# GLA joined to the attention and feed-forward block: one memory map, no barrier, its first steps beside the last feed-forward supertiles

## What is computed

```python
x = x + ln(attention(ln(x), qkv_w, qkv_b, out_w, out_b))
x = x + ln(ffn(ln(x), ternary(W1), b1, ternary(W2), b2))
x = x + ln(gla(ln(x), Wq, Wk, Wv, Wo, Wg, Wog, Wd, bd, norm_w))
x = x + ln(experts(ln(x), gate_W, W1, b1, W2, b2, Ws1, bs1, Ws2, bs2))

# inside gla: 16 heads of 64, sequences of 1024 tokens
log_decay = -softplus(x @ Wd.T + bd)
k_gated   = (x @ Wk.T) * sigmoid(x @ Wg.T)
s_t = exp(g_t) * s_{t-1} + k_t^T v_t ;  o_t = q_t s_t
out = rmsnorm(o) * norm_w * sigmoid(x @ Wog.T)  @ Wo.T
```

## Time and profile before

| | |
|---|---|
| median of 3 runs | 2134.86 us (2133.71 to 2137.86) |
| the profiled execution | 2135.97 us |
| its span in the trace | 2133.8 us |
| mean granted PE clock | 0.966 |
| PE / PEld busy | 94% / 66% |
| DVE / ACT / POOL busy | 71% / 60% / 28% |
| DMA | 176.5 MB, 83 GB/s on average |

### The profile page before, as it was taken

How to read it: one execution, slowest core, us unless ns; L and a number is a source line. 1 busy time by engine, 2 the same in 40 slices (tenths; PEclk the granted TensorE clock), 3 DMA queues, 4 the chain that set the end, 5 groups by cost and what they waited for, 6 DMA issues and landing times. The chain is left out here.

```text
span 2133.8 us, 42103 instructions
## 1 busy us (share of the span) xinstructions
PE 1996.7 (94%) x16914; PEld 1412.3 (66%) x16914; DVE 1519.0 (71%) x2461; ACT 1289.1 (60%) x2555; POOL 597.0 (28%) x481
## 2 busy tenths in 40 slices
PE   7999999999999997983899999999999999589997
PEld 6643333333333346972788888888888888478996
DVE  7889999999999966974465655555565554467774
ACT  3258888888888865763454545454545454255664
POOL 1200000000000024541333343434343433124454
PEclk9889999999999999995999999999999999879999
DMA  6732232232232222205212131212221212132221
GB/s 227 247 54 64 65 71 69 59 77 70 52 84 71 68 69 70 70 31 152 90 62 85 59 99 62 88 61 80 62 80 62 80 62 70 43 107 97 112 110 70
DMA packets 99410, 176.53 MB, mean 83 GB/s; under 512 B 24120, under 2 KB 61776, under 8 KB 94096
## 3 DMA queue, kind: packets, MB, share of 16 engines
q1 hardware_dynamic: 99216, 173.84, 26.8%
HBM read 134.35 MB, written 38.67 MB: 81 GB/s over the span
## 5 line engine op out<-in xcount | busy, mean ns | idle before, releaser
L731 DVE TENSOR_REDUCE att_sb_mx<-att_ps_psM 128x1 f32<-128x1024 f32 x512 | 624.1, 1221 | 27.6 <-PE att_ps_psM L944 24.9
L1149 ACT ACTIVATE att_sb_pt<-att_ps_psSO 128x512 f32<-128x512 f32 x1024 | 557.1, 597 | 94.5 <-PE att_ps_psSO L962 39.6
L944 PE MATMUL att_ps_psM<-stack_sb_k,stack_sb_q 48*128 48x512 f32 x1024 | 382.4, 455 | 4.9 <-DVE att_sb_mx L731 3.3
L962 PE MATMUL att_ps_psSO<-stack_sb_q,stack_sb_k 50*128 50x512 f32 x1024 | 373.5, 444 | 0.0
L974 PE MATMUL att_ps_psSO<-att_sb_pt,stack_sb_v 128*32 128x256 f32 x4096 | 326.4, 391 | 8.6 <-ACT att_sb_osb L1142 8.6
L962 PEld LDWEIGHTS att_ps_psSO<-stack_sb_q,stack_sb_k 50*128 50x128 f32 x1024 | 153.1, 185 | 201.8 <-ACT att_sb_pt L1149 155.5
L974 PEld LDWEIGHTS att_ps_psSO<-att_sb_pt,stack_sb_v 128*32 128x32 f32 x4096 | 82.0, 108 | 192.0 <-issue 102.5
L2190 ACT ACTIVATE gla_sb_sg<-gla_ps_psP 128x512 f32<-128x512 f32 x64 | 38.4, 600 | 258.8 <-PE gla_ps_psP L1965 258.8
L2407 DVE TENSOR_TENSOR gla_sb_dm<-gla_ps_psA,gla_sb_dm 128x512 f32<-128x512 f32 x128 | 82.3, 685 | 131.4 <-PE gla_ps_psA L2080 131.4
L2521 POOL TENSOR_TENSOR gla_sb_dm<-gla_sb_dm,gla_sb_masked 128x1024 f32<-128x1024 f32 x64 | 158.6, 2499 | 45.5 <-DMA gla_sb_dm<-decay_rows 45.5
L944 PEld LDWEIGHTS att_ps_psM<-stack_sb_k,stack_sb_q 48*128 48x128 f32 x1024 | 157.2, 190 | 19.1 <-DVE att_sb_mx L731 16.2
(11 more groups left out here) (261 smaller groups left out, 4568.2 us busy)
## 6 DMA issues: line engine op xcount, KB each, us to landing
gla_sb_dm<-decay_rows SPq DMA_DIRECT2D x32, 1024.0 KB, 5.2
qk_parts<-stack_sb_part SPq DMA_DIRECT2D x32, 512.0 KB, 3.2
gla_sb_eg<-decay_exp SPq DMA_DIRECT2D x64, 256.0 KB, 6.2
moe_sb_gb<-gate_rows SPq DMA_DIRECT2D x8, 2048.0 KB, 7.8
stack_sb_q<-qk_parts SPq DMA_DIRECT2D x192, 64.0 KB, 2.9
stack_sb_k<-qk_parts SPq DMA_DIRECT2D x96, 128.0 KB, 4.5
att_sb_rb<-sums SPq DMA_DIRECT2D x32, 256.0 KB
attended<-att_sb_on SPq DMA_DIRECT2D x32, 256.0 KB, 4.8
```

The source lines that it names most:

```text
L731: nc.vector.tensor_reduce(mx[:, qh, 8 * r + c:8 * r + c + 1], psM[:, t % 2, :], AX.X, ALU.max).then_inc(maxima_taken, 1)
L944: mm = pe.matmul(psM[:, t % 2, c * ST:(c + 1) * ST], q[rs, g, qh, j, n * P:(n + 1) * P], k[rs, g, j, c * ST:(c + 1) * ST], start=True, sto ...
L962: pe.matmul(psS[:, ring_slot(pos), :], k[rs, g, j, s * P:(s + 1) * P], q[rs, g, qh, j, :], start=True, stop=True).then_inc(ring_done, 1)
L1149: nc.scalar.activation(pt[:, s % (LAG + 2), ORDER[i], :], psS[:, (pos + 1) % 3, :], ACT.Exp, scale=AD ** -0.5).then_inc(ring_taken, 1)
```

## The change

`phase_gla` becomes `gla_programs`, which returns for each engine its pieces as functions; `phase_attention_ffn_gla` calls them from inside its own engine programs. The slots of GLA, its matmuls and its other arithmetic stay as they are; what changes:

- **Memory.** GLA's tiles are laid by hand over dead tiles of attention and the feed-forward part (`Area`). Each weight has its own raw, high and low tile, where the raw one lies under the low one; nothing is staged through q and og. The normed x overwrites xin, and xin has one buffer where it had two: at slot 2 SP loads x a second time for the residual (`x_again`). PSUM is shared by views of the same 8 banks.
- **No barrier** between the feed-forward part and GLA; the first weights, constants and x are loaded during feed-forward supertile 3 and later.
- **Weights are split by halves** (128x1024), `high` and `low` of wg and wk inside feed-forward supertiles 5, 6 and 7.
- **Norm, turn, logits, keys** of GLA's supertile 0 stand inside feed-forward supertiles 4 to 7 and beside `y_part(7)`.
- **Two moves at the start of the feed-forward part:** the last DVE reciprocal goes up behind `split_hidden(0, 0)`, the last POOL normalize goes up before `split_hidden(0, 5)`.
- **`wo` is scaled** by POOL after the first masks and weigh_keys, no longer before them.

```diff
 @block.sync (after the attention units)
@@ -714,10 +718,16 @@
                 if i + 4 < NST:
                     sp.wait_ge(f_.a_done, i + 3)
                     attended(i + 4)
-            for i in (NST - 2, NST - 1):
-                out(i)
+                if i == 3:
+                    gla_first()
+            gla_values()
+            gla_rows()
+            out(NST - 2)
+            gla_more()
+            out(NST - 1)
             for s in f_.x_outd:
                 sp.wait_ge(s, 16 * NST // 2)
+            gla_rest()
 @block.vector
             split_hidden(0, 0)
+            reciprocal(2 * NBG - 1, 1)
             normalize_x1(1)
...
             split_hidden(0, 6)
-            reciprocal(2 * NBG - 1, 1)
             add_projected(2)
 
             for i in range(1, NST):
                 split_hidden(i, 0)
                 if i + 1 < NST:
                     stats_of_x1(i + 1)
+                if i == NST - 1:
+                    gla_turned(0)
                 split_hidden(i, 2)
...
                 take_y(i - 1, 0)
+                if i == NST - 1:
+                    gla_turned(1)
                 split_hidden(i, 4)
...
+                if i in (NST - 2, NST - 1):
+                    gla_low(i - (NST - 2), 0)
                 split_hidden(i, 6)
...
+                if i == 2:
+                    gla_set()
+                if i == 5:
+                    gla_clear()
+                if i == 4:
+                    gla_stats()
+                if i == NST - 2:
+                    gla_norm()
+                    gla_low(0, 1)
+                    gla_low_heads()
+            gla_low(1, 1)
+            gla_keys()
             add_y(NST - 2)
+            gla_decays()
             take_y(NST - 1, 0)
             take_y(NST - 1, 1)
             stats_of_y(NST - 1)
+            gla_columns()
             add_y(NST - 1)
+            gla_queries()
+            gla_rest()
 @block.tensor
+                    if i == NST - 1 and f in (1, 4):
+                        gla_turn(f // 4)
+                    if i == NST - 1 and f == FT - 1:
+                        gla_logits()
                 if i:
                     y_part(i - 1, NT - 1, 1)
+            gla_keys(0)
             for n in range(NT):
                 for part in range(2):
                     y_part(NST - 1, n, part)
+            gla_keys(1)
+            gla_values()
+            gla_rest()
 @block.scalar
+                    if i in (NST - 3, NST - 2) and f in (1, 4):
+                        gla_high(i - (NST - 3), f // 4)
+                    if i == NST - 2 and f == 5:
+                        gla_heads()
+                    if i == NST - 1 and f in (1, 4):
+                        gla_turned(f // 4)
                 if i + 2 < NST:
                     shift_xin(i + 2)
+            gla_gates()
             shift_x1(NST - 2)
+            gla_values()
             shift_x1(NST - 1)
+            gla_queries()
+            gla_rest()
 @block.gpsimd
                 split_hidden(i, 3)
-                split_hidden(i, 5)
                 if i == 0:
                     normalize(BATCH - 1, NG - 1, 1)
+                split_hidden(i, 5)
...
+                if i == 5:
+                    gla_root()
+                if i == NST - 2:
+                    gla_state()
             norm_of_y(NST - 1)
+            gla_masks()
+            gla_rest()
```

More of the change, by code:

```diff
@@ L1943, in body @@
[L1943 to L1945 removed]
+                if not last:
+                    sp.wait_ge(turned, KD * (i + 1))
+                    sp.wait_ge(f_.x_outd[1 - u], 16 * ((i + 1) // 2 + 1))
+                    sp.dma_start(xin[:, :, :], xv[i + 1]).then_inc(x_in, 16)
+            if n == 2:
+                if not last:
+                    sp.wait_ge(turned, KD * (i + 2))
+                sp.dma_start(xin[:, :, :], xv[i]).then_inc(x_again, 16)
@@ L1947, in _, with body, rest @@
+        def body(i, u, last):
+            for n in range(NC):
+                slot(i, u, n, last)
+        def rest():
             each_supertile(sp, body)
@@ new lines, in slot @@
+            scores(0)
+            from_state()
+            if n == 2 and not last:
+                decay_inputs(i + 1, 1 - u)
+            if ahead:
+                gate(*nxt, 0)
+                key(*nxt, 0)
+            update()
+            if n % 2:
+                out_project(c - 1)
+            scores(1)
+            if n == 3 and not last:
+                decay_columns(i + 1)
+            if ahead:
+                gate(*nxt, 1)
+                key(*nxt, 1)
+                keys_turned(nxt[0], nxt[2], 0)
@@ L2153, in _, with first_turn, first_logits @@
+            for g in range(2):
+                from_chunk(g)
+            if ahead:
+                keys_turned(nxt[0], nxt[2], 1)
+                for h in range(2):
+                    values(*nxt, h)
+            if n % 2 and ahead:
+                half_supertile(nxt[0], nxt[1], nxt[2] // 2, c, n == 1 and not last)
+        def first_turn(k):
+            if k == 0:
+                pe.wait_ge(f_.a_taken, NT * NST)
+            turn_in(0, k)
+        def first_logits():
             pe.wait_ge(wd_ready, 1)
```

1335 lines of the change are left out of this document (681 added, 654 removed).

## The result

The changed kernel takes 2088.68 us (median of 4 runs, 2087.83 to 2089.38), the kernel before 2135.14 (4 runs). The ratio is 0.9781, with a 95% interval of 0.9764 to 0.9798: 46.5 us less. It was forecast 2083, with a range of 2074 to 2100.

A forecast was written before the change was run, and what follows sets the result against it. PE was taken to bound the feed-forward and GLA stretches, so gains come where PE is not full. Start 9 plus tail 43 makes 52 off the profiled 2135.97, 2084, or 2083 against the median; range 2074 to 2100.

The forecast's parts named there:

- What bounds, and that a gain passes through: PE fills the feed-forward and GLA stretches; time won ahead of them passes whole to the program's end.
- Term A: Start of the feed-forward part: earlier reciprocal and normalize cut PE's 11.87 us idle; 9 us gain, bounds 7.3 and 10.3.
- the 1.4 us of clock: Start of the feed-forward part: with a shorter PE idle gap, the loss from matmuls at the lower clock goes too.
- The feed-forward part between: Middle feed-forward supertiles: added casts, low parts, statistics and norm beside a full PE; 1.0 us charged in all.
- The chain up to `half_supertile`: From y of supertile 6 through GLA's prologue: `half_supertile` begins at 975.2, not 1020.56; 50.2 us less for the stretch.
- the wait of 3.9 us: Feed-forward's end, at 950.2: PE's first keys wait for wk's last low part, with `y_part(7)` queued behind.
- `half_supertile` itself: GLA's prologue up to chunk 0: takes 15.07 us plus 1.6 for ACT's high part of wog ahead of its copies.
- POOL's chain: GLA's prologue: masks, keys, `wo` twice and masks take POOL 22.5 us; chunk 0's second pair charged 0.7 us.
- Rival 1: GLA's prologue: DVE instructions wait for POOL's running one, costing 8 us beside the path; 2091, chance 0.16.
- Rival 3: Serial tail: late wog, lower clock and table loads cut the prologue's gain to 30 us; 2096, chance 0.07.
- Rivals 2 and 4: First: another instruction cancels the start's gain, 2092, chance 0.07. Second: single-buffered x delays each GLA supertile, 2165, chance 0.04.
- term B: Feed-forward's end to GLA's first chunk: early loads, casts and no barrier; 43 us gain, bounds 30 and 48.

The follow-up runs named there:

- the kernel with the queries first: Changed kernel with ACT's copies of all four query pairs and half the decay exponentials ahead of wog's high part: 2090.56 us.

## Why the prediction was right, and where it was off

- **What bounds, and that a gain passes through:** right. PE fills both long stretches as before, and the gains of the tail and of the start add up to the span.
- **Term A:** 8.1 for 9. The step that was off is the 1.4 us of clock on top of the shift's lead, "with a short gap that goes too": it did not go. In eight of the nine profiles with 0.50 for the first matmul, PE's clock fell to the lower level within 1 us of that matmul's start, and y(0) comes 10.9 us behind it as before the change. In those eight the shift comes 18.3 to 18.4 us behind the attention's end and not 26.5, so it leads by 8.1 to 8.3, inside the 7.3 to 8.9 forecast, and A is that lead and nothing else. The changed kernel's own profile reaches the same 8.1 another way: the fall lies ahead of the wait, PE's projection took 4.54 us there and not 3.62, DVE idled 1.22 for ACT behind it, the statistics were complete at 805.8 and the shift led by 6.5 only; then no fall followed, and PE had 1.5 us of that back. DVE also stood 1.68 us at the denominators' landing, at 792.8 where 790.9 was forecast, but that is not what made the shift late: other profiles wait for it up to 1.34 us with the statistics as early as in the rest. Two profiles have both falls, and A is 5.6 there.
- **The feed-forward part between:** its 1.0 us of charge was not there. y of supertile 4 came 6.6 us earlier than before and not 8.0, that of supertile 5 8.1 earlier again (from 820 to 941 PE idled 1.8 us in all); the turns, logits and waits of the last one took 3.8.
- **The chain up to `half_supertile`:** forecast 50.2, measured 49.3 less. Its steps came as said: the wait of 3.9 us was 4.07, and the start, 975.2 less the 8.05 of A, is 967.1, measured 967.07. But the wait does not set that start, as the prediction had it: with the keys behind `y_part(7)` it is gone, and `half_supertile` begins 26.45 us behind y(6), not 25.91. That part of the path was wrong, and the number did not suffer by it.
- **`half_supertile` itself** is the term that was mis-sized: +1.6 forecast, +5.2 measured. The order of events was there (ACT's high part of wog ahead of the query copies), but wog was put down as landed at 977.5 - 8 = 969.5 and came at 973.7. I had taken the issue and landing of the kernel before; here these 8 loads were issued right behind the output of supertile 6 and the decay broadcasts, in a stretch with 260 GB/s (961.4 to 969.5; 159 in that of before), took 8.12 us to issue, not 4.22, and 7.0 each to land, not 2.6. Issued earlier, in the kernel with wog first, they took 4.22 and 2.8 again.
- **POOL's chain** was not 0.7 late but in time: wo arrived late as well (POOL idle 5.63), yet the masks had begun at 965.96, where 975.4 - 8 = 967.4 was said, and PE is never idle in the first 100 us behind the first scores. The stretch to the end is 0.6 longer all the same, somewhere behind; where was not found.
- **Rival 1** was not at work on the path of the changed kernel: its 3.79 us residual was off it. That is luck in part: POOL stood idle for wo until 978.35, and so was no neighbour to DVE's low parts of wog at 974.77. In the kernel with the queries first the two decayed queries did meet POOL's scalings and took 8.14 us. This rival became the bound as soon as wog was early: PE idled 4.75 us there. **Rival 3** held one part of its conditions, wog late, and was worth 3.6 and not 13. **Rivals 2 and 4** are shown false by the moves alone and by the third load of x.
- **The references:** where the prediction names for casts, table loads and POOL's groups, they stand in the earlier trace rows, and the timelines it takes from the earlier trace rows stand in the earlier trace rows. GLA's statistics (2.1), the turns (1.1), the logits (1.4), the 1.7 us of idleness and the times of the chain in term B are estimates; no row ahead of the prediction has them.

By the profiles 47.7 of the 52 came: 0.9 was missing in A, 0.9 in the chain and 3.6 in `half_supertile`, and 1.1 came back between, from charges that were not needed; that they make up for part of the rest is luck. The medians give 46.5, since the profiled execution of before lies 0.8 above its median and that of after 0.4 below.

## What to carry to other kernels

When a prologue is laid beside the end of the phase before, its loads meet that phase's outputs and each other: take the issue and landing times of a load from a stretch with the traffic it will meet, and ask which engine's queue stands behind its wait. When a late load is repaired, look at once at what the two engines that share a port do in the time it frees: here the repair won 1 us until POOL's scaling of wo went to DVE, and 6 after. And a step that is moved behind others on SP is a load moved too; reordering won 7.4 us up to `half_supertile`, and one load that had slipped behind an output took 4.5 of them back.
